# Hand-written instruction orders of a fused attention and feed-forward kernel: one order for every batch in place of a repeated period

## What is computed

```python
def _L0_xattn_ref(x, context, mask, W_q, W_k, W_v, W_o, b_o):
    q = (x @ W_q).reshape(b, n, HEADS, DIM_HEAD)      # 8 heads of 64
    k = (context @ W_k).reshape(b, j, HEADS, DIM_HEAD)
    v = (context @ W_v).reshape(b, j, HEADS, DIM_HEAD)
    sim = jnp.einsum('bihd,bjhd->bhij', q, k) * scale
    sim = jnp.where(mask[:, None, None, :], sim, max_neg)
    attn = jax.nn.softmax(sim, axis=-1)
    out = jnp.einsum('bhij,bjhd->bihd', attn, v).reshape(b, n, INNER)
    return out @ W_o + b_o
def bitlinear(x, w, b):
    return jnp.einsum('bsd,fd->bsf', act_quant(rmsnorm(x)), weight_quant(w)) + b
# the feed-forward block: h = bitlinear(x, w1, b1); h = gelu(h); bitlinear(h, w2, b2)
x = x + tanh(g_xattn[0]) * _L0_xattn_ref(_layernorm(x), ctx_768, mask, W_q, W_k, W_v, W_o, b_o)
x = x + tanh(g_ffn[0]) * _L0_ffn_ref(_layernorm(x), w1, b1, w2, b2)
```

## Time and profile before

| what | us |
|---|---|
| median of three executions | 1063.77 |
| span of the profiled execution | 1062.5 |
| PE busy in it | 1011.3 |
| ACT, DVE, POOL busy | 846.1, 818.6, 765.7 |
| first matmul begins | 15.2 |

### The profile page before, as it was taken

The page is one execution under the profiler, slowest core; times in us unless marked ns, Lnnn a source line. Parts: engine busy times, 40 slices in busy tenths (PEclk is TensorE's granted clock), DMA queues, the critical chain, the costliest instruction groups (busy, mean ns, idle before and its releaser), DMA issues.

```text
span 1062.5 us, 24267 instructions
## 1 busy us (share of the span) xinstructions
PE 1011.3 (95%) x8576; PEld 600.3 (56%) x8576; DVE 818.6 (77%) x1774; ACT 846.1 (80%) x1458; POOL 765.7 (72%) x743
## 2 busy tenths in 40 slices
PE   4989999999999999999999999999999999999877
PEld 2556555556555655656565566656555556566433
DVE  4697988868788777878868777887868767797866
ACT  4878686987969769796978878797896977789766
POOL 4498987677766778776776787777686687787751
PEclk9999999999999999999999999999999999999999
DMA  8599898886978888796887988788896799678760
GB/s 264 198 208 243 140 203 152 162 161 141 172 139 159 160 167 165 140 170 138 171 166 134 169 149 166 143 175 163 147 171 128 148 180 177 127 129 146 132 122 31
DMA packets 472135, 168.83 MB, mean 159 GB/s; under 512 B 450384, under 2 KB 452176, under 8 KB 471632
## 3 DMA queue, kind: packets, MB, share of 16 engines
q1 hardware_dynamic: 472016, 167.29, 80.8%
HBM read 48.09 MB, written 7.34 MB: 52 GB/s over the span
## 4 chain that ended last, share of the span: by engine, by line
PE 75%; POOL 8%; ACT 6%; DMA 5%; issue 3%; DVE 2%; SPq 0%; POOLq 0%; ACTq 0%; DVEq 0%
PE ps_g L647 41%; PE ps_s L677 10%; PE ps_g L704 9%; PE ps_g L743 7%; PE ps_g L780 7%; DMA pt<-p 4%; POOL p L1199 3%; PE ps_g L692 1%; POOL p L1194 1%; ACT prob L1042 1%; POOL ctx L1210 1%; ACT hq L1158 1%; ACT h_sb L1148 1%; ACT p L1049 1%; POOL attn L1205 1%
## 5 line engine op out<-in xcount | busy, mean ns | idle before, releaser
L1199 POOL TENSOR_TENSOR p<-prob,p 112x750 f16<-112x750 f32 x256 | 405.8, 1596 | 94.3 <-ACT p L1049 92.0
L862 DVE CUSTOM_DVE_ANT_0 prob<-ps_s,mbias 112x750 f32<-112x750 f32 x256 | 236.7, 936 | 63.0 <-PE ps_s L677 54.8
L1042 ACT ACTIVATE prob<-prob,rmin 112x750 f32<-112x750 f32 x256 | 232.7, 912 | 5.7 <-DVE rmin L862 5.3
L647 PE MATMUL ps_g<-ctx,wk 128*128 128x375 f16 x1152 | 200.8, 326 | 18.3 <-POOL ctx L1210 16.4
L647 PE MATMUL ps_g<-wv,ctx 128*128 128x512 f16 (+1 forms) x864 | 196.5, 379 | 0.0
L647 PEld LDWEIGHTS ps_g<-ctx,wk 128*128 128x128 f16 x1152 | 110.3, 98 | 101.1 <-issue 27.0
L677 PE MATMUL ps_s<-k_sb,q_sb 64*112 64x375 f16 x1536 | 149.8, 327 | 7.4 <-DVE rmin L862 7.4
L1049 ACT ACTIVATE p<-prob 112x750 f16<-112x750 f32 x160 | 127.9, 820 | 18.7 <-DMA pt<-p 18.1
L647 PEld LDWEIGHTS ps_g<-wv,ctx 128*128 128x128 f16 (+1 forms) x864 | 86.3, 103 | 94.4 <-issue 5.2
L704 PE MATMUL ps_g<-pt,v_sb 128*64 128x224 f16 (+1 forms) x2448 | 123.2, 255 | 9.2 <-DMA pt<-p 9.2
L677 PEld LDWEIGHTS ps_s<-k_sb,q_sb 64*112 64x112 f16 x1536 | 90.0, 126 | 60.0 <-issue 35.5
(11 more groups left out here) (134 smaller groups left out, 1462.4 us busy)
## 6 DMA issues: line engine op xcount, KB each, us to landing
ctx_f<-in_ctx SPq DMA_DIRECT2D x47, 375.0 KB, 3.9
xa<-in_x SPq DMA_DIRECT2D x16, 448.0 KB, 4.6
xr<-in_x SPq DMA_DIRECT2D x28, 256.0 KB, 3.0
out<-xr SPq DMA_DIRECT2D x28, 256.0 KB, 2.6
pt<-p SPq DMA_TRANSPOSE x256, 4.2
h_sb<-in_w SPq DMA_DIRECT2D x4, 512.0 KB, 8.3
w<-in_w SPq DMA_DIRECT2D x3, 512.0 KB, 5.4
xr<-in_w SPq DMA_DIRECT2D x3, 512.0 KB, 11.2
```

The costliest lines, as they stand in the source:

```text
L647: mm = nc.tensor.matmul(out, lhs, rhs, start=(m == 0), stop=(m == len(steps) - 1))
L862: nc.vector.tensor_tensor_reduce(prob[:, (b * NU + n) % PROBS, :].rearrange("p (c k) -> p c k", c=2), ps_s[0:HT, n % 2, :, 0:CH], mbias[:, ...
L1042: nc.scalar.activation(prob[:, (b * NU + n) % PROBS, :], prob[:, (b * NU + n) % PROBS, :], ACT.Exp, bias=rmin[:, n:n + 1], scale=-1.0, acc ...
L1199: nc.gpsimd.tensor_tensor(p16[:, u % HILO, 1, 0:J], prob[:, (b * NU + n) % PROBS, :], p16[:, u % HILO, 0, 0:J], ALU.subtract).then_inc(s[" ...
```

## The change

The period and the function that repeats it are gone. Each of the five lists is written out for all 16 batches. Each list holds the same pieces as before, each once (496 on SP, 670 on PE, 1071 on ACT, 993 on DVE, 628 on POOL); only their order differs, in the start, the middle and the end. The code that emits a piece is unchanged, and the ring of banks follows the new order of PE. The new lists are not periodic: each batch has an order of its own.

```diff
-def sequence(engine):
-
-    start, cycle, end = ORDERS[engine]
-    return start + [(kind, n, i + later) for i in range(FIRST, LAST) for kind, n, later in cycle
-                    if exists(kind, n, i + later)] + end
-
-
-SP_SEQ, PE_SEQ, ACT_SEQ = sequence("SP"), sequence("PE"), sequence("ACT")
-DVE_SEQ, POOL_SEQ = sequence("DVE"), sequence("POOL")
+def in_order(text):
+
+    return [(kind, int(n), int(b)) for kind, n, b in (token.split(":") for token in text.split())]
```

The starts of the lists of PE, ACT and POOL:

```diff
 PE
-    K:0:0 K:1:0 K:2:0 K:3:0 K:4:0 Q:0:0 Q:1:0 Q:2:0 S:0:0 V:0:0 V:1:0 V:2:0 S:1:0 K:5:0 K:6:0 K:7:0 V:3:0 V:4:0
-    V:5:0 S:2:0 S:3:0 Q:3:0 WM:0:0 S:4:0 K:0:1 V:0:1 V:1:1 S:5:0 PV:0:0 V:2:1 V:3:1 S:6:0 K:1:1 K:2:1 K:3:1
+    K:0:0 K:1:0 K:2:0 K:3:0 K:4:0 K:5:0 K:6:0 Q:0:0 S:0:0 V:0:0 V:1:0 S:1:0 V:2:0 V:3:0 V:4:0 V:5:0 Q:1:0 Q:2:0
+    K:7:0 S:2:0 S:3:0 S:4:0 Q:3:0 WM:0:0 PV:0:0 S:5:0 V:0:1 V:1:1 V:2:1 K:0:1 S:6:0 K:1:1 V:3:1 Q:0:1 K:2:1 K:3:1
 ACT
-    CX:0:0 PW:0:0 CX:1:0 CX:2:0 XH:0:0 XH:1:0 PW:1:0 K:0:0 K:1:0 K:2:0 K:3:0 PW:2:0 WA:0:0 K:4:0 Q:0:0 Q:1:0
-    Q:2:0 WA:1:0 WA:2:0 E:0:0 E:1:0 V:0:0 V:1:0 V:2:0 H:0:0 XH:0:1 XH:1:1 WA:3:0 K:5:0 K:6:0 H:1:0 WA:4:0 E:2:0
-    K:7:0 E:3:0 WA:5:0 H:3:0 V:3:0 V:4:0 CX:0:1 CX:1:1 V:5:0 E:4:0 WA:6:0 H:4:0 WA:7:0 CX:2:1 Q:3:0 E:5:0 E:6:0
+    CX:0:0 PW:0:0 CX:1:0 CX:2:0 XH:0:0 K:0:0 XH:1:0 K:1:0 K:2:0 K:3:0 K:4:0 PW:1:0 PW:2:0 WA:0:0 K:5:0 K:6:0 Q:0:0
+    V:0:0 E:0:0 V:1:0 WA:1:0 E:1:0 H:0:0 E:2:0 E:3:0 H:1:0 H:3:0 V:2:0 V:3:0 V:4:0 Q:1:0 WA:2:0 Q:2:0 CX:0:1 E:4:0
+    V:5:0 H:4:0 XH:0:1 XH:1:1 WA:3:0 WA:4:0 CX:1:1 CX:2:1 K:7:0 WA:5:0 WA:6:0 WA:7:0 E:5:0 PW:3:0 E:6:0 E:7:0 Q:3:0
 POOL
-    CX:0:0 N1:0:0 CX:1:0 CX:2:0 MB:0:0 N1:0:1 L:0:0 L:1:0 H:2:0 L:2:0 L:3:0 CX:0:1 CX:1:1 L:4:0 CX:2:1 WB:0:0
-    WB:1:0 WB:2:0 H:5:0 L:5:0 L:6:0 WB:3:0 H:7:0 WB:4:0 N1:0:2 L:7:0 L:8:0 H:10:0 WB:5:0 PL:0:0 L:9:0 L:10:0
+    N1:0:0 CX:0:0 CX:1:0 CX:2:0 MB:0:0 L:0:0 L:1:0 H:2:0 N1:0:1 L:2:0 CX:0:1 L:3:0 CX:1:1 CX:2:1 L:4:0 H:5:0 WB:0:0
+    L:5:0 WB:1:0 WB:2:0 H:7:0 N1:0:2 L:6:0 L:7:0 L:8:0 WB:3:0 L:9:0 H:10:0 WB:4:0 L:10:0 WB:5:0 L:11:0 PL:0:0 H:13:0
...
```

On DVE the split of the Q weights moves from ahead of KL:2:0 to behind KL:4:0, and the low part of Q:0:0 stands behind the split of the V weights:

```diff
-    N1:0:0 XN:0:0 PW:0:0 XH:0:0 XH:1:0 KL:0:0 KL:1:0 PW:1:0 KL:2:0 KL:3:0 PW:2:0 QL:0:0 KL:4:0 QL:1:0 QL:2:0
+    N1:0:0 XN:0:0 PW:0:0 XH:0:0 KL:0:0 XH:1:0 KL:1:0 KL:2:0 KL:3:0 KL:4:0 PW:1:0 PW:2:0 QL:0:0 M:0:0 M:1:0 KL:5:0
...
```

On SP the four turns that the last PV of batch 0 needs, and those of the second PV of batch 4 (the period stood for that batch before):

```diff
-    T:12:0 WL:12:0 T:13:0 T:14:0 WL:13:0 T:15:0 T:0:1 WL:14:0 WL:15:0 LC:2:2 XT:0:2 XT:1:2 T:1:1 T:2:1 T:3:1
+    XT:0:1 WL:8:0 T:6:0 XT:1:1 WL:10:0 T:8:0 T:7:0 WL:9:0 T:9:0 WL:11:0 T:10:0 T:11:0 LR:1:0 LC:1:2 T:12:0 WL:12:0
+    T:14:0 WL:13:0 T:15:0 T:13:0 WL:14:0 WL:15:0 LC:2:2 XT:0:2 XT:1:2 T:0:1 LC:0:3 T:1:1 LX:0:3 T:2:1 T:3:1 BD:1:0
...
-    XT:0:1 XT:1:1 LX:0:2 T:1:0 T:2:0 T:3:0 XQ:0:-1 T:4:0 T:5:0 T:6:0 T:7:0 XQ:1:-1 LR:0:0 LR:1:0 LC:0:2 T:8:0
+    LR:1:4 XT:1:5 XT:0:5 T:2:4 T:1:4 T:3:4 LX:0:6 LC:1:6 XQ:0:3 F2:1:2 T:4:4 LR:0:5 T:5:4 T:7:4 T:8:4 T:6:4 XQ:1:3
...
```

One batch of the middle on PE, the period and what stands for a batch now:

```diff
-    PV:3:-1 Q:3:0 S:3:0 O:0:-1 O:1:-1 S:4:0 Q:0:1 Q:1:1 V:0:1 V:1:1 K:0:1 F1:0:-1 F1:1:-1 F1:2:-1 F1:3:-1 K:1:1
-    PV:0:0 S:5:0 V:2:1 V:3:1 K:2:1 K:3:1 S:6:0 PV:1:0 K:4:1 F1:4:-1 F1:5:-1 F1:6:-1 F1:7:-1 S:7:0 V:4:1 K:5:1
-    V:5:1 S:0:1 F2:0:-1 PV:2:0 S:1:1 K:6:1 K:7:1 Q:2:1 S:2:1 F2:1:-1
+    Q:2:11 V:4:11 V:5:11 S:2:11 F2:1:9 PV:3:10 S:3:11 Q:3:11 O:0:10 O:1:10 Q:0:12 Q:1:12 V:0:12 V:1:12 S:4:11
+    F1:0:10 F1:1:10 F1:2:10 F1:3:10 K:0:12 K:1:12 S:5:11 PV:0:11 V:2:12 K:2:12 S:6:11 K:3:12 V:3:12 F1:4:10 F1:5:10
+    K:4:12 F1:6:10 F1:7:10 PV:1:11 S:7:11 K:5:12 V:4:12 V:5:12 F2:0:10 K:6:12 S:0:12 PV:2:11 S:1:12 K:7:12 Q:2:12
+    S:2:12 F2:1:10
...
```

385 lines of the change are left out of this document (242 added, 143 removed).

## The result

Four executions of the kernel after took 1107.53 to 1114.56 us, median **1111.87**; the kernel before, run beside it, 1063.62. The ratio is 1.0450, with a 95% interval of 1.0414 to 1.0486: slower by 48 us, where 1063 was forecast. The profiled execution is the fastest of the four: it took 1107.53 us, its span 1105.3. Where the others spent up to 7 us more, no trace shows. Lines of the code have moved down by 86 (L611 is now L697).

What follows compares the result with a forecast made beforehand. PE was taken as the bound, busy 1011.3 of 1062.5 us, with another engine pacing the first 170 us. Start +1.0, entries -2.4, middle's waits +0.8 and end 0 gave -0.6 on 1063.8: 1063 us, range 1053 to 1076.

Steps and rivals of the forecast that it cites:

- The middle's waits: Batches 2 to 12: places with under 2.5 us of cover rise from 3 to 21; +0.8 us, 0 to 16 possible.
- The start: First 170 us, walked through the new lists up to L:15:1: +1.0 us, between 1.7 earlier and 3.8 later.
- step 1: Start: K:0 to K:6 and one Q precede S:0:0, which starts at 32.2 in place of 28.8, 3.4 us later.
- Step 3: Start, POOL's work from L:6:0 (ends 73.8) to L:15:0: 22.2 us plus 2.1 for longer L, ending at 98.1, before 94.8.
- The walk: The start traced piece by piece through the new lists; wrong if L:15:0 ends before 95 or after 102 us.
- Step 5: Start, PL:3:0 to L:15:1: 47.1 us of POOL work, old 45.8; 1.7 us earlier to 3.8 later, +1.0 taken.
- The entries: Middle, PE entering S or PV from a full piece: 112 become 88, at 0.10 us each, -2.4 us.
- The end: From 985 us PE's order is nearly the old one: 0, give or take 3 us.
- The clock: Start: a longer idle stretch between Q:3:0 and WM:0:0 might slow PE's clock, 1.4 us by rule; left out of the sum.
- The slower one: Rival: PE waits in batches 2 to 12 for late take-outs, 18 places at 0.9 us; 1078.6 us, chance 0.30.
- The faster one: Rival: new lists fill better from 60 us on, halving PE's idle time to 170 us; 1051.5 us, chance 0.32.
- the order does not matter: Rival: PE's work is fixed, all else hidden, only its entries show; 1061.4 us, inside the forecast's case, chance 0.38.

Runs made afterwards that it cites:

- a_no_ffn_turns: New lists, low part of the probabilities computed for 375 of 750 columns, no XQ and HT issued for tiles 2 to 24; 1069.17 us, 1.0079 of the kernel before.

## Why the prediction was wrong, point by point

**The middle's waits: the step that failed.** The text took "each of 443 places" where a PE piece needs a bank or the scores' place, counted those with under 2.5 us of cover, and came to +0.8, with 16 as the far end. PE's idle time in the middle grew by 27.9 us. The kind of wait that was counted grew by 9.1 of that (0.8 to 9.9 us from 190 to 1000 us), inside the far end of 16 but not near +0.8. The main fault is what the count left out, put at nothing without a reason: the turned operands, for which PE waits 16.8 us and not 2.4. T:6:4 behind T:8:4 was called "one issue or two" inside the same bound, 1.5 to 3 us; such a T waits for the later unit's L and came 3.5 us later on average. The cover of T, XQ and HT, in SP's list and in POOL's, was never laid along the lists, and without XQ and HT and half of L all but 5.7 of the 32.9 us go. Each unit goes S, M, E, H, L, T, PV, with a queue at each step, and the buffers feed the delay back (M waits for L of five units before, H for the turn of four before). Of the earlier trace rows I read that PE is busy 99.6% of the middle and took the margin of the others for granted; busy shares of 72 to 80% tell nothing of how late each piece may be. Which single distances in the new lists shrank below what a step takes was not found; no run mends the middle with all of its work in place.

**The start, +1.0; it measured +11.4 at PV:3:1** (and +1.4% of the time, some 15 us, in the exchange of the starts). The early steps held in their times: S:0:0 at 31.8 (32.2 given), S:2:0 at 50.1 (50.4), L:4:0 ending at 64.3 (64.0). For S:0:0 that is in part luck: the first matmul came 0.9 later, which no step had, and step 1 itself then cost 2.1 and not 3.4. Step 3 failed. By its own rows it also adds too much for the longer L: 9 x 0.15 is 1.4, not 2.1. POOL's timeline of after, L:6:0 to L:15:0:

```profile
69.57 3.15 POOL L1269 TENSOR_SCALAR hq<-hq,winv 128x1024 f32<-128x1024 f32 x1
...
75.15 4.54 POOL L1285 TENSOR_TENSOR p<-prob,p 112x750 f16<-112x750 f32 x3
...
84.95 2.78 POOL L1285 TENSOR_TENSOR p<-prob,p 112x750 f16<-112x750 f32 x1
...
91.53 1.51 POOL L1285 TENSOR_TENSOR p<-prob,p 112x750 f16<-112x750 f32 x1 [2.70 <-ACT p L1135]
...
98.60 1.93 POOL L1285 TENSOR_TENSOR p<-prob,p 112x750 f16<-112x750 f32 x1 [0.50 <-ACT p L1135]
...
103.42 1.61 POOL L1285 TENSOR_TENSOR p<-prob,p 112x750 f16<-112x750 f32 x1
```

L:6:0 ended near 76.7 (the first of three L from 75.15), 2.9 later than given, 2.0 of it in one WB that took 3.15 and not 1.12, beside DVE's split of the output weights (68.44 to 71.73; see the last section). L:15:0 ended at 105.0, not 98.1: the other 4.0 are 3.4 of waits (2.70, 0.20, 0.50) in a stretch that I had filled with work alone, and longer instructions. "The walk is wrong if L:15:0 ends [...] after 102" was the test, and it says so. The main matmuls of PV:3:0 began at 112.8 (105 given, 102.3 before), 10.5 later and not 2.5. Step 5 failed too: from PL:3:0 to L:15:1 it is 53.9 us, where the old took 51.3 and the step gave 47.1 to 52.6, so L:15:1 ended at 171.3 (157 to 163 given) and PV:3:1 began 11.4 later. No step has what PE shows in this stretch, 13.0 us of waits for the scores' place and the low clock behind them.

**The entries, -2.4:** not seen. The lists have 24 entries less, as counted. PE's busy time between the marks rose by 5.0 in after. Where waits are nearly gone it is 806.16 in the new order (a_no_ffn_turns) and 805.85 in the old: 0.3 more, not 2.4 less. The price of 0.10 an entry, read from two places, did not carry over to the count.

**The end, 0 give or take 3:** right, -1.5 (87.0 us from PV:3:14 on, 88.5 before). **The clock:** 0.98 from 100 to 170 us in both, as in the earlier trace rows, but 0.95 and not 1.00 in the first 100 us. The text looked to the idle stretch between Q:3:0 and WM:0:0 and expected POOL's pace to cover it; the drop came with the waits for the scores' place ahead of S:3:0, and the sum had nothing for it.

**The rivals.** The slower one had the right sign, but its place, the released bank and the scores' place, holds 9.1 of the 27.9 us, and its 1078.6 us fell short by 33. The faster one fell with the start. That the order does not matter fell most clearly of all: the 14 kernels with the same work took from 1064 to 1171 us.

## What to carry to other kernels

Where several in-order lists feed each other through small rings of buffers, a list has no value of its own: the same order of 42 turns cost about 4 us among one set of lists and 67 among the other. Before pricing a new order, lay every producer-to-consumer distance along all lists, the DMA issue queue's above all, and compare it with the measured delay of that step; a list that waits in order also holds back what stands behind the wait. Where one engine is busy over 99%, small waits on many pieces add up (1.4 to 1.7 us for each piece moved), and waits that lower the clock cost once more in matmul time. Single pieces moved back mended nothing here, but a whole stage could be exchanged: the old start before the new lists won back what the new start had cost.

## What was not expected of the hardware

A DVE instruction with two inputs in SBUF can stand still while POOL works back to back. DVE's XH of batch 14 in after, with the instruction that O:1:13 waited for, 3.1 us:

```profile
959.93 4.99 DVE L997 SCALAR_TENSOR_TENSOR xh<-xa,rs,xh 112x512 f16<-112x512 f32 x1 [1.16 <-ACT xh L1172]
...
965.14 0.73 DVE L1095 SCALAR_TENSOR_TENSOR xr<-ps_g,smh,xr 128x512 f32<-128x512 f32 x1
```

and POOL's instructions beside it:

```profile
959.92 1.51 POOL L1285 TENSOR_TENSOR p<-prob,p 112x750 f16<-112x750 f32 x1
961.39 2.98 POOL L1296 TENSOR_TENSOR ctx<-ctx_f,ctx 128x750 f16<-128x750 f32 x2
964.34 3.52 POOL L1285 TENSOR_TENSOR p<-prob,p 112x750 f16<-112x750 f32 x2
```

The median XH takes 0.76 us. This one ended 0.55 after the third POOL instruction did (the second CX, at 964.37), so by its length it made no progress beside any of the three; the L behind it took 2.05 and not 1.5. The other long XH show the same sum, POOL's remaining time plus 0.55 (2.00 us beside 1.45 left of a CX; in before 2.09 beside 1.54). That XH of 2.00 us, at 60.8, got in between two POOL instructions that followed without a wait, and POOL's L then took 2.06; so POOL does not always keep DVE out. In before the longest took 3.21 us, but there the F2 take-out stood ahead of it and nobody waited. It can go the other way: POOL's WB at 69.57 took 3.15 us and not 1.12, and ended 1.0 after DVE's split of the output weights beside it had (71.73). The split of wk at the start took 6.06 us in after beside POOL's three CX, and the first matmul came at 16.1 in place of 15.2. The Trainium skill, SBUF — State Buffer, section on the two separate sides, has the port pair that VectorE and GpSimd share as an exclusive lock held for a whole instruction; the traces agree, and add that instructions of POOL that follow one another without a wait can keep the pair: three did here, while at 60.8 us the next one did not. What this costs the change as a whole was not measured by itself; DVE's busy time is 2.6 us higher in all.
